# Vision tower of two layers: order of the second attention, of its value products and of the fillers, changed

## What is computed

```python
h = tok(x)
h = h + attn0(layernorm(h))   # random-feature attention, 12 heads, causal sums
h = h + ffn0(layernorm(h))    # 32 experts, 4 picks a token, gelu, hidden 768
h = h + attn1(layernorm(h))   # rotary positions, 12 heads of 16, causal softmax
h = h + ffn1(layernorm(h))    # 8 experts, 2 picks a token, and one shared; silu gate
```

```python
q = rope(X @ Wq + bq)
k = rope(X @ Wk + bk)
v = X @ Wv + bv
scores = einsum('bqhd,bkhd->bhqk', qh, kh) / sqrt(hd)
weights = softmax(where(causal, scores, -inf), axis=-1)
out = einsum('bhqk,bkhd->bqhd', weights, vh)
```

## Time and profile before

| | |
|---|---|
| three runs, us | 308.32, 307.76, 309.35 |
| the profiled execution, us | 308.32 |
| its span, first to last instruction, us | 306.5 |
| mean granted TensorE clock, share of full | 0.953 |
| TensorE matmul (PE) busy | 280.7 us, 92% of the span |
| VectorE (DVE) busy | 154.1 us, 50% |
| ScalarE (ACT) busy | 112.4 us, 37% |
| chain that ended last: PE, DVE, DMA | 72%, 10%, 10% |

### The profile page before, as it was taken

How to read it: one execution, slowest core, us unless ns; L and a number is a source line. 1 busy time by engine, 2 the same in 40 slices (tenths; PEclk the granted TensorE clock), 3 DMA queues, 4 the chain that set the end, 5 groups by cost and what they waited for, 6 DMA issues and landing times.

```text
span 306.5 us, 7468 instructions
## 1 busy us (share of the span) xinstructions
PE 280.7 (92%) x2634; PEld 186.5 (61%) x2634; DVE 154.1 (50%) x431; ACT 112.4 (37%) x386; POOL 64.2 (21%) x76
## 2 busy tenths in 40 slices
PE   7989997879999999999999999964797999989994
PEld 6948976636566565665655655644676887355543
DVE  0565676545565544445545532300576844754454
ACT  1155250304535536345354354350232646211100
POOL 5500000322224334243252241120250000000000
PEclk9999999669999999999999999995899799799999
DMA  7992009828999999999999999637700000000001
GB/s 271 384 411 89 2 5 351 351 59 316 336 401 409 405 405 410 404 406 410 404 407 405 404 404 404 256 129 251 306 0 3 4 0 2 0 0 0 2 0 51
DMA packets 19960, 70.94 MB, mean 231 GB/s; under 512 B 3617, under 2 KB 4838, under 8 KB 19792
## 3 DMA queue, kind: packets, MB, share of 16 engines
q1 hardware_dynamic: 17328, 65.62, 55.2%
q0 software_dynamic: 2304, 3.68, 3.5%
q10 hardware_dynamic: 288, 1.13, 0.9%
HBM read 68.97 MB, written 3.28 MB: 236 GB/s over the span
## 4 chain that ended last, share of the span: by engine, by line
PE 72%; DVE 10%; DMA 10%; issue 4%; ACT 2%; DVEq 1%; SPq 1%; POOLq 0%; ACTq 0%
PE ps L988 13%; PE ps L946 10%; PE ps L951 5%; PE ps L965 5%; DMA x_rows<-xn_rows,row_ids 5%; PE ps L1070 4%; PE ps L1058 4%; PE ps L763 3%; PE ps L1025 3%; DMA attn_rows<-in_attn_rows 3%; PE ps L1061 2%; PE ps L936 2%; PE ps L770 2%; PE ps L750 1%; PE ps L928 1%
## 5 line engine op out<-in xcount | busy, mean ns | idle before, releaser
L653 ACT ACTIVATE turned<-ps,route_in 128x64 f32<-128x64 f32 x288 | 61.4, 340 | 72.9 <-PE ps L965 72.8
L500 POOL DMA_INDIRECT x_rows<-xn_rows,row_ids x24 | 25.2, 1048 | 113.8 <-DVE row_ids L1265 112.9
L1279 DVE COPY probs<-ps 128x768 f32<-128x768 f32 x24 | 23.0, 957 | 23.8 <-PE ps L951 23.8
L512 POOL DMA_INDIRECT y_picks<-fexp,row_ids x24 | 24.3, 1011 | 27.2 <-DVE fexp L1364 17.1
L988 PE MATMUL ps<-late_in,turned 128*64 128x192 f32 x216 | 26.0, 329 | 1.2 <-ACT turned L653 1.2
L988 PE MATMUL ps<-expert_w,turned 128*64 128x192 f32 x288 | 25.8, 329 | 0.0
L988 PEld LDWEIGHTS ps<-late_in,turned 128*64 128x64 f32 x216 | 19.0, 137 | 5.0 <-ACT turned L653 1.8
L965 PE MATMUL ps<-cst,probs 128*128 128x128 f32 x144 | 21.1, 281 | 0.9 <-DVE probs L1279 0.9
L988 PEld LDWEIGHTS ps<-expert_w,turned 128*64 128x64 f32 x288 | 19.3, 137 | 3.8 <-ACT turned L653 0.6
L1364 DVE COPY fexp<-ps 128x192 f32<-128x192 f32 x24 | 8.6, 357 | 24.6 <-PE ps L988 24.6
L946 PE MATMUL ps<-expert_w,fexp 128*64 128x384 f32 x96 | 19.4, 527 | 0.8 <-DVE fexp L1268 0.6
(11 more groups left out here) (240 smaller groups left out, 466.4 us busy)
## 6 DMA issues: line engine op xcount, KB each, us to landing
expert_w<-in_experts SPq DMA_DIRECT2D x48, 576.0 KB, 12.6
late_in<-in_experts SPq DMA_DIRECT2D x36, 576.0 KB, 12.0
probs<-in_experts SPq DMA_DIRECT2D x12, 576.0 KB
late_in<-in_ffn_in SPq DMA_DIRECT2D x1, 2592.0 KB, 12.9
probsT<-in_patches SPq DMA_DIRECT2D x4, 384.0 KB, 7.0
qk_padT<-y_picks SPq DMA_DIRECT2D x4, 384.0 KB, 5.0
late_in<-in_attn_in SPq DMA_DIRECT2D x1, 864.0 KB, 4.3
attn_w<-in_attn_w SPq DMA_DIRECT2D x1, 673.5 KB, 9.0
```

Of the source, the lines that this page charges most:

```text
L500: pool.indirect_dma_start(out=x_rows[:, x_u, :], out_offset=None, in_=xn_rows, in_offset=bass.IndirectOffsetOnAxis(ap=row_ids[:, u % STEPS ...
L512: pool.indirect_dma_start(out=y_picks, out_offset=bass.IndirectOffsetOnAxis(ap=row_ids[:, u, 1:2], axis=0), in_=y_rows[:, u % RING, :], in ...
L653: last = act.activation(hidden[:, u % 2, half * (KH // 2) + c, slots_of(q)], ps[:, 4 + half, c * P + q * SLOTS:c * P + (q + 1) * SLOTS], A ...
L1279: dve.tensor_copy(raw.rearrange("p (h n) -> p h n", h=2), ps[:, 2:4, 0:HID // 2]).then_inc(raw_sb, 1)
```

## The change

1. `weigh` runs over the pairs of heads outside and the two images inside, in both attentions.
2. Six fillers instead of one ahead of the pick products; three of 128 columns between them and the token transposes.
3. Second attention: the values first, after all four copies of `xnT`; then three query-key products, two head transposes, the fourth product. VectorE rotates straight from the bank, cosines included; ScalarE's copy to `turned` and GpSimd's product are gone. ScalarE copies the values and, ahead of them, computes one exponential into `exp_table`. One mask product a bank serves two tiles; the score products run over the row groups innermost. Banks are renumbered.
4. The first `gate_product` of the last layer stands in the middle of the choice of experts.

```diff
@@ -518,13 +519,6 @@
                     for u in range(IDS_AHEAD):
                         gather(0, u, True)
                     rounds(pool, send)
-                else:
-
-                    for t in range(NT):
-                        pool.wait_ge(qk_sb, t + 1)
-                        pool.tensor_tensor(fexp[:, t].rearrange("p h f -> p (h f)").rearrange("p (m n) -> p m n", m=2),
-                                           turned[:, t].rearrange("p (m n) -> p m n", m=2),
-                                           const("rope_cos").unsqueeze(1).to_broadcast([P, 2, D]), ALU.mult).then_inc(rope_cos_part, 1)
 
...
@@ -597,14 +591,17 @@
 
             def attention_1():
 
-                for t in range(NT):
-                    act.wait_ge(qk_mm, NT + t + 1)
-                    act.copy(turned[:, t], ps[:, t, 0:2 * D]).then_inc(qk_sb, 1)
-                for t in range(NT):
+                def heads_turned(t):
+
                     act.wait_ge(qk_padT_mm, NT + t + 1)
                     bank = TURN_BANK[1][t]
                     act.copy(qk_padT[:, t].rearrange("p (b j) n -> p b (j n)", b=2), ps[:, bank:bank + 2, 0:HB * P]).then_inc(qk_padT_sb, 1)
 
+                act.activation(exp_table[:, :], const("ln_eps"), ACT.Exp)
+                values_out(1, (0, 1))
+                for t in range(NT):
+                    heads_turned(t)
+
                 def exponents(t):
 
...
@@ -756,11 +753,11 @@
                     pe.wait_ge(scores_read, t + 1)
                 else:
                     pe.wait_ge(probsT_sb, t + 1)
-                for b in range(IPT):
-                    for g in range(2):
-                        for j in range(HB):
-                            pair = 2 * j + g
-                            last = nc.tensor.matmul(ps[b * SEQ:(b + 1) * SEQ, OUT_BANK[t], pair * 2 * VW:(pair + 1) * 2 * VW],
+                for g in range(2):
+                    for j in range(HB):
+                        pair = 2 * j + g
+                        for b in range(IPT):
+                            last = nc.tensor.matmul(ps[b * SEQ:(b + 1) * SEQ, OUT_BANK[a][t], pair * 2 * VW:(pair + 1) * 2 * VW],
                                                     probsT[:, t, pair if a else g * HB + j, b * SEQ:(b + 1) * SEQ], v_bd[:, IPT * t + b, pair, :], start=True, stop=True)
                 last.then_inc(att_mm, 1)
...
@@ -822,28 +819,29 @@
 
             def attention_1():
 
+                def queries_and_keys(t):
+
+                    rows, cols = slice(0, DB + 1), slice(t * P, (t + 1) * P)
+                    nc.tensor.matmul(ps[:, t, 0:2 * D], xnT[:, 0, cols], wqkv1[:, 0, 0:2 * D], start=True, stop=False)
+                    nc.tensor.matmul(ps[:, t, 0:2 * D], xnT[rows, 1, cols], wqkv1[rows, 1, 0:2 * D], start=False, stop=True).then_inc(qk_mm, 1)
+
                 def turn(t):
 
                     pe.wait_ge(qk_pad_ready, NT + t + 1)
-                    if t == 1:
-                        pe.wait_ge(qk_sb, 2)
-                    elif t == 2:
-                        pe.wait_ge(qk_sb, NT)
-                    elif t == 3:
-                        pe.wait_ge(qk_padT_sb, NT + 1)
                     turn_heads(1, t)
 
+                def masks(t):
+
+                    for i in range(HG):
+                        nc.tensor.matmul(ps[:, SCORE_BANK[t] + i, :].rearrange("p (u n) -> p u n", u=2)[:, :, 0:HB * SEQ], ident16[:, :],
+                                         future16[:, :, :].rearrange("p j k -> p (j k)").unsqueeze(1).to_broadcast([P, 2, HB * SEQ]), start=True, stop=False, skip_group_check=True)
+
                 def scores(t):
 
-                    pe.wait_ge(qk_padT_sb, NT + (3 if t < 2 else NT))
-                    if t == 2:
-                        pe.wait_ge(v_sb, 8)
-                    bank, at = t // 2 * HG, t % 2 * (BANK // 2)
-                    for i in range(HG):
-                        nc.tensor.matmul(ps[:, bank + i, at:at + HB * SEQ], ident16[:, :], future16[:, :, :].rearrange("p j k -> p (j k)"), start=True, stop=False, skip_group_check=True)
-                    for i in range(HG):
-                        for j in range(HB):
-                            for b in range(IPT):
+                    bank, at = SCORE_BANK[t], t % 2 * (BANK // 2)
+                    for j in range(HB):
+                        for b in range(IPT):
+                            for i in range(HG):
                                 rows, cols = slice(i * HPAD, (i + 1) * HPAD), slice(b * SEQ, (b + 1) * SEQ)
                                 last = nc.tensor.matmul(ps[b * SEQ:(b + 1) * SEQ, bank + i, at + j * SEQ:at + (j + 1) * SEQ],
                                                         qk_padT[rows, t, j, cols], qk_padT[rows, t, HB + j, cols], start=False, stop=True, skip_group_check=True)
...
+                values_with_bias_row(wqkv1[:, :, 2 * D:3 * D])
+                for t in range(NT - 1):
+                    queries_and_keys(t)
                 turn(0)
-                values_with_bias_row(wqkv1[:, :, 2 * D:3 * D])
                 turn(1)
-                turn(2)
+                queries_and_keys(NT - 1)
                 pe.wait_ge(mask_ready, 2)
+                pe.wait_ge(v_sb, 8)
+                pe.wait_ge(qk_padT_sb, NT + 1)
+                masks(0)
+                pe.wait_ge(qk_padT_sb, NT + 2)
                 scores(0)
                 scores(1)
+                turn(2)
                 turn(3)
+                pe.wait_ge(qk_padT_sb, 2 * NT)
+                masks(2)
                 scores(2)
                 scores(3)
...
@@ -1017,7 +1024,7 @@
             pe.wait_ge(combT_sb, 4)
             for t in range(NT):
                 nc.tensor.matmul(ps[:, 2 * t, 0:D], combT[:, t * P:(t + 1) * P], b2_rows[:, :], start=True, stop=False)
-            keep_busy(1, 7)
+            keep_busy(6, 7)
             pe.wait_ge(pick_diag_ready, NT)
             for t in range(NT):
                 pe.wait_ge(y_back_dma[t], 16)
@@ -1025,13 +1032,10 @@
                     last = nc.tensor.matmul(ps[:, 2 * t, 0:D], pick_diag[:, k, t, :], y_back[:, t, k, :], start=False, stop=(k == PICKS - 1))
                 last.then_inc(picks_mm, 1)
 
+            keep_busy(3, 7, P)
             turn_tokens(2)
             pe.wait_ge(attn1_dma, 16)
-            for t in range(NT):
-                rows, cols = slice(0, DB + 1), slice(t * P, (t + 1) * P)
-                pe.wait_ge(xnT_sb, 2 * NT + (NT if t == 3 else t + 1))
-                nc.tensor.matmul(ps[:, t, 0:2 * D], xnT[:, 0, cols], wqkv1[:, 0, 0:2 * D], start=True, stop=False)
-                nc.tensor.matmul(ps[:, t, 0:2 * D], xnT[rows, 1, cols], wqkv1[rows, 1, 0:2 * D], start=False, stop=True).then_inc(qk_mm, 1)
+            pe.wait_ge(xnT_sb, 3 * NT)
             attention_1()
 
             keep_busy(4, 1)
...
@@ -1375,20 +1379,21 @@
 
             def rotate(t):
 
-                x2 = turned[:, t].rearrange("p (a h r e) -> p a h r e", a=2, r=2, e=HD // 2)
+                x2 = ps[:, t, 0:2 * D].rearrange("p (a h r e) -> p a h r e", a=2, r=2, e=HD // 2)
                 s2 = rope_swap[:, t, 0:2 * D].rearrange("p (a h r e) -> p a h r e", a=2, r=2, e=HD // 2)
                 sin = const("rope_sin").rearrange("p (h r e) -> p h r e", r=2, e=HD // 2)
-                dve.wait_ge(qk_sb, t + 1)
+                dve.wait_ge(qk_mm, NT + t + 1)
+                step(dve.tensor_tensor(fexp[:, t].rearrange("p h f -> p (h f)").rearrange("p (m n) -> p m n", m=2), ps[:, t, 0:2 * D].rearrange("p (m n) -> p m n", m=2),
+                                       const("rope_cos").unsqueeze(1).to_broadcast([P, 2, D]), ALU.mult))
                 for r in range(2):
                     n = step(dve.tensor_tensor(s2[:, :, :, r], x2[:, :, :, 1 - r], sin[:, :, r].unsqueeze(1).to_broadcast([P, 2, H, HD // 2]), ALU.mult))
                 after(n)
-                dve.wait_ge(rope_cos_part, t + 1)
                 dve.tensor_tensor(qk_pad[:, t, :, 0:HD], fexp[:, t], rope_swap[:, t, 0:2 * D].rearrange("p (h f) -> p h f", f=HD), ALU.add).then_inc(qk_pad_ready, 1)
...
             def centre(t):
 
                 dve.wait_ge(scores_mm, NT + t // 2 * 2 + 2)
-                bank, at = t // 2 * HG, t % 2 * (BANK // 2)
+                bank, at = SCORE_BANK[t], t % 2 * (BANK // 2)
@@ -1396,7 +1401,6 @@
 
             for t in range(NT):
                 rotate(t)
-            values_out(1, (0, 1))
             for t in range(NT):
                 centre(t)
             normalise(1, 0)
@@ -1409,10 +1413,17 @@
             layer_norm(3)
+            def gate_product(n, u, first=False):
+                dve.wait_ge(silu_done, n + 1)
+                if not first:
+                    dve.wait_ge(down1_mm, n - 1)
+                dve.tensor_tensor(gated[:, u, :], silu[:, u, :], ps[:, 2 * u + 1, :], ALU.mult).then_inc(gated_ready, 1)
+
             dve.wait_ge(score_ready, 1)
```

(7 more changed lines are left out.)

22 lines of the change are left out of this document (9 added, 13 removed).

## The result

| | before | changed |
|---|---|---|
| median of four runs, us | 308.84 | 300.61 |
| runs, us | 308.32, 307.76, 309.35, 310.32 | 302.83, 300.62, 299.65, 300.60 |
| span of the profiled execution, us | 306.5 | 301.0 |

The ratio is 0.9709, 95% interval 0.9666 to 0.9753. The forecast was 300.1 us, 297.6 to 304.0. The profiled execution of the changed kernel is its slowest of four (302.83 us, mean granted clock 0.964, where the others have 0.971 to 0.977), so its span is 5.5 us shorter than before and not 8.2. Both numbers are needed to judge the terms. A *low clock spell*, or spell, is a stretch in which TensorE's granted clock is 0.50.

A forecast was written before the change was run, and what follows sets the result against it. The second attention was taken as mostly bound by TensorE's own queue, with low-clock stretches elsewhere. Terms -1.3 - 1.4 - 4.0 - 1.5 = -8.2 took 308.3 to 300.1 us, range 297.6 to 304.0.

The forecast's parts named there:

- the clock at the picks: Sign at the picks' read-back: granted clock 1.00, and the picks' last add at 217 less 1.3 us.
- A: Value products of both attentions, alternating partition halves: 0.66 us saved per tile, two first-attention tiles on the chain, -1.3 us.
- the 27 ns: Time per value-product record at 34 columns, taken between 46 and 16 ns: 0.65 us a tile.
- R3: Rival, value products: alternating gains nothing at 34 columns, by the page's rule; 303.1 us, chance 0.07.
- R1: Rival, routing: the clock falls earlier against the work, so A is +1.0, not -1.3; 302.4 us, chance 0.12.
- B: Picks' read-back: six fillers for one hold the clock, -1.4 us; -1.9 at full clock, 0 if it falls anyway.
- at full clock throughout: Case at the picks: transfers bound instead, last tile done at 217.1 instead of 219.0 us, -1.9.
- R2: Rival at the picks: six fillers don't hold the clock, so B is 0; 301.5 us, chance 0.12.
- C: Second attention rebuilt in its new order: ends at 250.65 instead of 254.66 us, -4.0; bounds -3.2 and -4.5.
- step 3: Second attention's masks and scores: 1.65 us for two tiles at 16 ns a record; probabilities' transposes 1.8 us sooner.
- D: Last feed-forward, first gate product earlier: -1.5 us, between -0.8 with the low clock and -2.5 where the clock holds.
- R4: Rival, second attention: gaps keep the clock down from 239 to 262 us; slower, 310.2 us, chance 0.04.

The follow-up runs named there:

- b1: Kernel before with six fillers ahead of the pick products and three small ones behind: ratio 0.9921 on six of twelve runs, 0.9985 by the median of all.
- d1: Kernel before with only the first gate product moved into the choice of experts: ratio 0.9924 to the kernel before.
- u_fillers: Changed kernel with one filler ahead of the picks as before and none of the three small ones: ratio 0.9797 to the kernel before.
- u_weigh: Changed kernel with the value products' old loop order, the two images outermost again: ratio 0.9824 to the kernel before.
- m2: Kernel before with alternating value products, row-groups-innermost scores, early gate product, added routing fillers, eleven pick fillers, three 256-column layer-norm fillers: ratio 0.9724.
- The second set of runs: The changed kernel, unchanged, timed again beside its own variants on one chip: ratio 0.9774 to the kernel before.

## Why the prediction was right, and where it was not

The median came out 0.5 us from the forecast. The terms did not all do so well, and one sign failed: the clock at the picks was not 1.00 but low from 211.1 to 218.0 us, and their last add came at 220.42 and not at 215.7.

- **A, first attention, -1.3.** Right in kind, too large: 24 records take 0.82 us (34 ns each) and not 0.65 (27 ns), and the choice comes 1.1 us sooner over fourteen profiles, 0.75 in the pair of profiles. The step that failed is the 27 ns, chosen between two rows without a reason for the place; the upper row (46 ns) and the lower (16 ns) held as bounds. R3, no gain from alternating, is refuted at 55 to 34 ns. Read as the prediction read it, the rule of the Trainium skill (TensorEngine Tiling (Array Packing), Instruction Overhead) not to take a tiling factor from a dimension that is already small would have given nothing here; the trace disagrees with that reading, with 0.49 us of 1.31 saved at 34 columns. The rule is about the size of tiles, and here the products are the same in both kernels: only their order changed.
- **R1, routing.** In the changed kernel's profile R is 1.1 us longer and the rival seems to have happened. It had not: the old value order shows the same R in b1 and d1 (15.02, 15.05), with the clock down from 54.0 and 54.4. What the new order gives back there is 0.3 us on average, inside the scatter of 1.2, not the 2.3 of the rival.
- **B, picks, -1.4.** In proportion the term most off. Six fillers end at 209.1, the picks come at 212.1, and the clock falls in between or doesn't: P is 14.2 to 16.2 with six (mean 14.95, five profiles) and 14.8 to 16.0 with one (mean 15.50, six). So -0.55 on average, with a scatter in each group that is larger; in the first pair of profiles P was 0.4 longer. u_fillers gave about 0.7 us, and b1 between 0.5 and 2.5, by which of its runs are counted. The step that failed is the price: with the clock at full throughout, P was 14.24 and so 1.3 below the mean with one filler, where the text had 1.9, and that came in one profile of five; in the other four the clock was low for 3.4 to 6.9 us, and P 1.0 below that mean at best and 0.7 above it at worst. "They delay nothing" held; "at full clock throughout" held for six fillers in u_weigh (14.24), where the picks came 7.8 us after the last copy. R2 is half true. The small fillers cost nothing, as forecast, and do nothing that shows.
- **C, second attention, -4.0.** Measured -4.3 from the last add of the picks to the last projection (35.60 to 31.26), and by the steps: waiting for all four copies +0.72 (0.4 forecast, because the first product had begun at 221.90 by its first record and not 222.06, and the last copy to the first value product is 0.14 more); the stage up to the third row maximum -2.77 at full clock; the value products -1.0 (-1.3 forecast); the rest, 0.33 in S and 0.96 in T, is the low clock at 240.3 to 243.7 us in the kernel before, which I had at 0.8. VectorE's centring bounds T as forecast, at 3.95 in all thirteen profiles behind the first. In the eight with the new value order TensorE is idle for 0.6 to 0.7 us ahead of it; in the five with the old one its queue ends at the same moment. What I had not seen is that the score products' loop order alone holds 1.27 of the 2.77: I priced the 16 ns a record in step 3 and put it to the account of the whole stage.
- **D, gate product, -1.5.** Bounds right, choice wrong: -2.53 at full clock, -0.89 under a spell, where the text had -2.5 and -0.8. G was 11.75 in eight of the nine profiles with the early gate product. VectorE's stall was 0.60 us in the changed kernel and 2.13 in m2; the second gate product was ready in time in both (266.27 + 0.69 before 267.76, 268.13 + 0.69 before 269.55).
- **R4** did not come near; no low spell between 226 and 262 us in the changed kernel.
- **The sum.** Terms at full clock now: -1.1 + 0.3 - 0.55 + 0.72 - 2.77 - 1.0 - 2.53 = -6.9 us. The second set of runs gave 309.17 - 302.33 = -6.8, the first -8.2. That the forecast of -8.2 met the first is partly luck: A was too large by 0.5, B by 0.85 and, against these terms, C by 0.95 (it was measured against a stage that had a spell in it); D was too small by 1.0; and a spell less is worth 1.6.
